# Many-head cross-attention: order of the work ahead of the bundles; expert layer: place of one wait

## The reference

```python
def _L1_ffn_ref(x, uzman_embeddings, W1, b1, W2, b2, onbellek_durumu):   # 8 experts, hidden 512
    sim = tokens @ uzman_embeddings.T                 # the best 7 of 8 experts by sim ...
    scores = einsum('nld,nd->nl', local_embs, t_norm) + 0.1 * onbellek_durumu[local_idx]
    top_scores, top_local = top_k(scores, 2)          # ... and of them the best 2 by score
    weights = softmax(top_scores)
    h = gelu(einsum('nd,edh->enh', tokens, W1) + b1)
    out_all = einsum('enh,ehd->end', h, W2) + b2      # weighted sum of the two chosen

def _L2_xattn_ref(query, key, value, mask, W_q, W_k, W_v, W_o):          # 16 heads of 8
    Q, K, V = _split(query @ W_q.T), _split(key @ W_k.T), _split(value @ W_v.T)
    scores = einsum('bhqd,bhkd->bhqk', Q, K) / sqrt(8)
    scores = where(mask, -inf, scores)                # one mask of 64 x 1601 for all batches
    out = einsum('bhqk,bhkd->bhqd', nan_to_num(softmax(scores)), V)
    return merged(out) @ W_o.T
```

## Time and profile before

| What | Value |
|---|---|
| Time, median of 3 runs | 3037.8 us (3036.95 to 3038.14) |
| The profiled execution: own time / span | 3035.62 us / 3033.8 us |
| Busy: PE, DVE, ACT, POOL | 86%, 67%, 46%, 14% of the span |
| Mean granted clock of PE | 0.928 |
| Expert layer | 713.1 to 973.8 us of the span |
| Many-head stage | 974.1 to about 2196 us of the span |

### The profile page before, as it was taken

One profiled execution on the slowest core, in us unless ns is written; L12 is line 12 of the kernel. 1 busy time (PEld: TensorE's weight loads), 2 busy tenths in 40 slices (PEclk: granted clock), 3 DMA queues, 4 the chain that ended last, 5 costly groups with the idle time before them and its releaser, 6 DMA issues. The chain is left out here.

```text
span 3033.8 us, 66495 instructions
## 1 busy us (share of the span) xinstructions
PE 2614.7 (86%) x26984; PEld 1711.9 (56%) x27014; DVE 2036.0 (67%) x6815; ACT 1385.4 (46%) x2520; POOL 429.6 (14%) x299
## 2 busy tenths in 40 slices
PE   7998645898998999999999999999947989888634
PEld 5767543555776666656556565555624555555423
DVE  5553514675212499999989999899667876556776
ACT  3441312564333255555555555555338964334511
POOL 0000030440000000000000000000005960563200
PEclk9999776898999999999999999999978999999866
DMA  7970410000001000000000001000002210991000
GB/s 235 332 245 3 130 48 19 9 3 17 15 22 37 22 24 23 27 32 24 23 24 24 23 24 34 24 23 2 5 12 79 96 58 1 325 366 66 2 0 14
DMA packets 73344, 189.00 MB, mean 62 GB/s; under 512 B 12130, under 2 KB 39717, under 8 KB 73008
## 3 DMA queue, kind: packets, MB, share of 16 engines
q1 hardware_dynamic: 64912, 156.68, 15.8%
q10 hardware_dynamic: 7104, 26.23, 2.4%
q0 software_dynamic: 1024, 1.85, 0.2%
HBM read 154.19 MB, written 30.79 MB: 61 GB/s over the span
## 5 line engine op out<-in xcount | busy, mean ns | idle before, releaser
L3062 DVE CUSTOM_DVE_ANT_0 L_xattn_junk<-L_xattn_ps_mx,L_xattn_shift 128x512 f32<-128x512 f32 (+1 forms) x1024 | 545.1, 570 | 112.3 <-issue 102.1
L3143 ACT ACTIVATE L_xattn_pT<-L_xattn_ps_st 128x512 f32<-128x512 f32 x768 | 417.0, 594 | 402.4 <-PE L_xattn_ps_st L2901 402.4
L2914 PE MATMUL L_xattn_ps_mx<-L_xattn_kT,L_xattn_qb 32*128 32x512 f32 (+1 forms) x2048 | 480.0, 551 | 0.0
L2901 PE MATMUL L_xattn_ps_st<-L_xattn_qb,L_xattn_kT 32*128 32x256 f32 (+1 forms) x3328 | 454.5, 383 | 0.0
L3108 DVE TENSOR_TENSOR L_xattn_pT<-L_xattn_pT,L_xattn_capT 128x512 f32<-128x512 f32 (+1 forms) x710 | 423.2, 637 | 29.8 <-ACT L_xattn_pT L3143 26.8
L2901 PEld LDWEIGHTS L_xattn_ps_st<-L_xattn_qb,L_xattn_kT 32*128 32x128 f32 (+1 forms) x3328 | 299.3, 180 | 18.5
L2961 PE MATMUL L_xattn_ps_pv<-L_xattn_pT,L_xattn_v 128*17 128x128 f32 x6656 | 263.0, 276 | 0.0
L2961 PEld LDWEIGHTS L_xattn_ps_pv<-L_xattn_pT,L_xattn_v 128*17 128x17 f32 x6656 | 146.1, 96 | 163.3 <-issue 76.1
L2927 PE MATMUL L_xattn_ps_st<-L_xattn_less,L_xattn_ones_b 3*128 3x512 bf16 x768 | 177.8, 385 | 0.9 <-ACT L_xattn_pT L3143 0.7
L2868 POOL TENSOR_TENSOR L_xattn_qb<-ln_sq,L_xattn_four 128x256 f32<-128x256 f32 x32 | 19.6, 615 | 1089.0 <-PE L_xattn_ps_st L2901 1069.3
L2914 PEld LDWEIGHTS L_xattn_ps_mx<-L_xattn_kT,L_xattn_qb 32*128 32x128 f32 x2048 | 151.5, 183 | 23.9 <-DVE L_xattn_tops L3062 14.6
(11 more groups left out here) (615 smaller groups left out, 5030.4 us busy)
## 6 DMA issues: line engine op xcount, KB each, us to landing
L_xattn_ctxT<-context_turned SPq DMA_DIRECT2D x64, 800.5 KB, 6.5
context_turned<-L_xattn_ctxT SPq DMA_DIRECT2D x32, 800.5 KB, 9.7
L_xattn_ctx<-in_ctx SPq DMA_DIRECT2D x32, 768.0 KB
L_xattn_ctx<-in_ctx ACTq DMA_DIRECT2D x32, 768.0 KB
L_attn_cc<-scratch_rows SPq DMA_DIRECT2D x32, 512.0 KB, 3.7
L_xattn_out_keys<-scratch_q SPq DMA_DIRECT2D x32, 200.1 KB, 10.0
L_ffn_w<-in_L_ffn_w SPq DMA_DIRECT2D x4, 1024.0 KB, 10.2
L_ffn_w<-in_L_ffn_W SPq DMA_DIRECT2D x16, 256.0 KB, 3.2
```

Of the source, the lines that this page charges most:

```text
L2901: last = nc.tensor.matmul(st[0:chunk[j], w % 3, 256 * c2:256 * c2 + 256], kT[n % 3][r:r + 32, P * j:P * j + chunk[j]], qb[n % 3][r:r + 32, ...
L2914: last = nc.tensor.matmul(mx[:, w % 3, to:to + width], qb[n % 3][32 * g:32 * g + 32, 2 * (p % 2):2 * (p % 2) + 2, :].rearrange("p h q -> p ...
L3062: last = nc.vector.tensor_tensor_reduce(out=junk[:, w % 3, to:to + width], in0=mx[:, w % 3, to:to + width], in1=shift[:, k0:k0 + width], s ...
L3143: nc.scalar.activation(pT[b % HELD][:, :, gi, :], st[:, w % 3, :].rearrange("p (c k) -> p c k", c=2), ACT.Exp)\
```

## The change

In the expert layer VectorE's wait for `loaded`, with the `bonus` multiplication behind it, stands behind `ln_vector` and no longer ahead of it.

In the many-head stage VectorE's part of the normalisation and the four query reads stand ahead of the wait for `loaded` and the mask work; "set" is now its last step ahead of the loop. TensorE makes the eight units of batch 0 directly behind the query products, in a loop of their own over four PSUM banks (the three of `st`, and `pv`) with a wait only for the unit four back, and only then the transposes of `cap`. ScalarE copies the eight units ahead of `capT`. The loop of bundles starts at -18 on the three engines. Nothing is computed in another way.

```diff
@@ routed_experts, vector
             nc.vector.memset(ones[:, :], 1.0).then_inc(V.did("ones"), 1)
+            ln_vector(c, dve, V, A, PE, tp)
             dve.wait_ge(loaded, 80)
             nc.vector.tensor_scalar(bonus[:, :], te[:, :], 0.1, None, ALU.mult).then_inc(V.did("bonus"), 1)
-            ln_vector(c, dve, V, A, PE, tp)
@@ many_head_cross_attention
+        FIRST_BATCH = [(PREPARED[i][0], 0, PREPARED[i][1]) for i in sorted(PREPARED)]
+        four_banks = [st[:, 0, :], st[:, 1, :], st[:, 2, :], pv[:, :]]
@@ tensor
-            pe.wait_ge(*V.at("q3"))
+            pe.wait_ge(ctx_in[0], 16)
+            for i, (kind, _, m) in enumerate(FIRST_BATCH):
+                bank = four_banks[i % 4]
+                if i >= 4:
+                    pe.wait_ge(prep_read, i - 3)
+                if kind == "V":
+                    for j in range(4 * m, 4 * m + part[m]):
+                        to = P * (j - 4 * m)
+                        last = nc.tensor.matmul(bank[0:chunk[j], to:to + P], ctxT[:, 0, P * j:P * j + chunk[j]], wv[:, :],
+                                                start=True, stop=True)
+                else:
+                    width = SPANS[m][1]
+                    last = nc.tensor.matmul(bank[:, 0:width], wk[:, :], ctxT[:, 0, 512 * m:512 * m + width], start=True, stop=True)
+                last.then_inc(prep_done, 1)
+            pe.wait_ge(*V.at("set"))
             pe.wait_ge(filled, 5)
+            pe.wait_ge(prep_read, 8)
             for j in range(KC):
                 last = nc.tensor.transpose(st[0:chunk[j], j // 8, S * (j % 8):S * (j % 8) + S], cap[0:S, P * j:P * j + chunk[j]],
                                           c.ident[0:S, 0:S])
...
-                    for _ in range(8 if b < -LEAD else 6):
+                    for _ in range(6):
...
-            for b in range(FIRST, LAST):
+            for b in range(-LEAD, LAST):
@@ vector
+            ln_vector(c, dve, V, A, PE, tp)
+            for i in range(4):
+                dve.wait_ge(*PE.at(f"q{i}"))
+                nc.vector.tensor_scalar(qT[:, 512 * i:512 * i + 512], qps[i], DH ** -0.5, None, ALU.mult).then_inc(V.did(f"q{i}"), 1)
             dve.wait_ge(loaded, 144)
...
             nc.vector.memset(zero_b[:, :], 0.0).then_inc(V.did("set"), 1)
-            ln_vector(c, dve, V, A, PE, tp)
-            for i in range(4):
-                dve.wait_ge(*PE.at(f"q{i}"))
-                nc.vector.tensor_scalar(qT[:, 512 * i:512 * i + 512], qps[i], DH ** -0.5, None, ALU.mult).then_inc(V.did(f"q{i}"), 1)
@@ scalar
-            act.wait_ge(*PE.at("capT"))
-            nc.scalar.copy(capT[:, 0:8, :], st[:, 0, :].rearrange("p (j q) -> p j q", q=S))
...
+            for unit in FIRST_BATCH:
+                taken(unit)
+            act.wait_ge(*PE.at("capT"))
+            nc.scalar.copy(capT[:, 0:8, :], st[:, 0, :].rearrange("p (j q) -> p j q", q=S))
...
-            for b in range(FIRST, LAST):
+            for b in range(-LEAD, LAST):
```

More of the change, by code:

```diff
@@ L2780, in many_head_cross_attention @@
         qps = [mx[:, 0, :], mx[:, 1, :], mx[:, 2, :], prep[:, :]]
-        V = Steps(s.sem("vector_steps"), (1, ["set"] + LN_V + [f"q{i}" for i in range(4)]))
+        V = Steps(s.sem("vector_steps"), (1, LN_V + [f"q{i}" for i in range(4)] + ["set"]))
         A = Steps(s.sem("scalar_steps"), (1, LN_A + ["capT"]))
@@ L2815, in many_head_cross_attention @@
         assert len(prep_at) == 12 * B
+        FIRST_BATCH = [(PREPARED[i][0], 0, PREPARED[i][1]) for i in sorted(PREPARED)]
+        assert [prep_at[unit] for unit in FIRST_BATCH] == list(range(1, 9))
+        four_banks = [st[:, 0, :], st[:, 1, :], st[:, 2, :], pv[:, :]]
         def of_bundle(b):
@@ L3154, in taken @@
                 width = SPANS[m][1]
+                bank = prep if n or kind == "M" else four_banks[FIRST_BATCH.index(unit) % 4]
                 if kind == "K":
-                    nc.scalar.copy(kT[n % 3][:, 512 * m:512 * m + width], prep[:, 0:width]).then_inc(prep_read, 1)
+                    nc.scalar.copy(kT[n % 3][:, 512 * m:512 * m + width], bank[:, 0:width]).then_inc(prep_read, 1)
                 elif kind == "V":
@@ L3159, in taken @@
                     nc.scalar.copy(v[n % 3][0:k, 4 * m:4 * m + part[m], :, 0:16],
[L3160 removed]
+                                   bank[0:k, 0:P * part[m]].rearrange("p (j h d) -> p j h d", j=part[m], d=16)).then_inc(prep_read, 1)
                 else:
                     nc.scalar.copy(less[n % 2][:, :, :], prep[:, 0:256].unsqueeze(1).broadcast_to([P, 2, 256])).then_inc(prep_read, 1)
[L3164 removed]
+            for unit in FIRST_BATCH:
+                taken(unit)
+            act.wait_ge(*PE.at("capT"))
+            nc.scalar.copy(capT[:, 0:8, :], st[:, 0, :].rearrange("p (j q) -> p j q", q=S))
+            nc.scalar.copy(capT[:, 8:12, :], st[:, 1, 0:4 * S].rearrange("p (j q) -> p j q", q=S))
+            nc.scalar.copy(capT[0:KREST, 12, :], st[0:KREST, 1, 4 * S:5 * S]).then_inc(A.did("capT"), 1)
+            for b in range(-LEAD, LAST):
                 now = of_bundle(b)
```

6 lines of the change are left out of this document (1 added, 5 removed).

## The result

| | before | after |
|---|---|---|
| Median (range; runs) | 3037.97 us (3036.95 to 3038.69; 4) | 3009.68 us (3008.67 to 3015.64; 4) |
| Profiled execution: own time / span | 3035.62 / 3033.8 us | 3009.04 / 3007.2 us |
| Mean granted clock | 0.928 | 0.931 |

The ratio is 0.9911, with a 95% interval of 0.9896 to 0.9927: faster by 28.3 us in the medians and 26.6 us in the profiled executions.

A forecast was written before the change was run, and what follows sets the result against it. TensorE fills the bundle loop, so the edits' worth is decided at two stage starts: 3.4 us (expert layer) plus 20.6 us (many-head) is 24.0, and 3037.8 - 24.0 = 3013.8 us; range 3010.5 to 3019.0, 8 in 10.

The forecast's parts named there:

- Expert layer: Expert layer's start: normalisation begins behind `ones`, not behind the load and `bonus`; 3.4 us earlier, bounds 0 to 3.5.
- Rival C: Expert layer: the edit gives nothing because another wait sets when the blocks start; 3017.2 us, chance 0.08.
- Normalisation ahead of the masks: Many-head stage's start: VectorE's normalisation starts 8.95 us earlier, less 0.7 us for GpSimd's fills beside its first tiles.
- the hold by the fills: Many-head normalisation: GpSimd's value-tile fills hold up VectorE's first normalised tiles by 0.7 us, bounds 0 to 2.3.
- Rival A: Many-head normalisation: the fills hold VectorE to their end, 2.3 us in place of 0.7; 3015.4 us, chance 0.13.
- Units in four banks: Many-head stage: units follow the last query product, 0.92 us per key and 0.96 per value unit; `cap` transposes 7.0 us later.
- Transposes and copies of cap: Many-head stage, now ahead of bundle -18: 2.13 us as before, with first maxima at 998.56.
- Bundles: Many-head loop: fourteen bundles with 112 fillers gone; from bundle -18 on TensorE's queue is row for row as before.
- Mask work beside the units: Many-head stage: the 2.67 us of mask work goes behind the query reads and runs beside TensorE's eight units.
- Rival B: Many-head queries and units: TensorE's low clock reaches into them, up to +9.3 us; whole 3023.1, half 3018.4; chance 0.12.
- Rival D: Queries, units and bundles from -18 on: slower, TensorE stays at the low clock; 42.1 us, time 3055.9, chance 0.02.

The follow-up runs named there:

- expert_only: The kernel before with only the expert layer's edit (normalisation ahead of the wait for the load and `bonus`): 3031.59 us, ratio 0.9981.
- pool_reads: The changed kernel with a GpSimd copy of 1536 columns of x, read by nobody, behind its first fill of the value tiles: 3006.14 us, one execution.
- norm_only: The kernel before with only VectorE's many-head order changed (normalisation and query reads ahead of the masks), one bank, bundles from -32: 3032.77 us, ratio 0.9988.
- banks_only: The kernel before with only the eight units moved ahead of `cap` in four banks, loop from bundle -18: 3029.19 us, ratio 0.9969.
- one_bank: The changed kernel with all eight units through one bank, each waiting for the copy of the one ahead: 3016.80 us, ratio 0.9927.
- pool_fills: The changed kernel with an extra GpSimd fill of 1536 columns, read by nobody, behind its first fill of the value tiles: 3012.64 us, one execution.
- pool_gap: The pool_reads kernel with GpSimd waiting behind its copy until VectorE's first pair of normalised tiles is written: 3014.02 us, one execution.

## Why the prediction was right, and where not

Direction, place and mechanism were right: two normalisations start at once, the units overlap the masks, and fourteen bundles of transposes go. The steps one by one, measured on the trace of after:

- *Expert layer*, 3.4 us: 3.5 in expert_only, so cost and place were right, and 4.0 in the changed kernel. The start is right (713.87, behind `ones`). From `ones` to the last copy it is 9.30 us (713.79 to 723.09) and was 13.58 (713.17 to 726.75); 3.5 of these 4.3 us are the start, and 0.8 is the clock, which rose some 3 us sooner in this trace than in seven others with the same code; 0.45 of it reaches the end of the layer. That part is luck. Rival C falls.
- *Normalisation ahead of the masks*, 8.95 us less 0.7: the first variances come at 0.03 us from the stage's start (9.05 before), and the last copy ends at 10.42 (19.67 before), 9.25 earlier, where 8.95 less 0.7 were forecast. The term that was mis-sized is the hold by the fills: 0.10, not 0.7, and by luck of phase. Rival A, the full hold, didn't happen in this kernel, but its mechanism is real: in pool_reads the tiles waited for every fill, and the first maxima came 3.0 us later.
- *Units in four banks*: the first at 14.69 us from the stage's start (15.38 forecast; of the 0.69 the hold is 0.6). Pitches are 0.86 us (K) and 0.89 (V), not 0.92 and 0.96: I had taken the time from a unit to the filler behind it, and from unit to unit it is shorter. To the transposes of `cap` it is 6.45 us, not 7.0. No bank was waited for.
- *Transposes and copies of cap*: 2.04, not 2.13.
- In sum the first maxima stand at 23.18, against 24.5 forecast: 21.95 us gained, not 20.6. The 1.3 us between are the hold (0.6), the units (0.55), `cap` (0.09), and 0.1 that I can't put down to one step.
- *Bundles*: 43.03 us from there in both. As forecast.
- *Mask work beside the units*: hidden, as forecast, but longer: the short pieces of `shift` and `cap` took 0.61 us each (0.19 before), and GpSimd's three `qb` 3.86 (1.75 before). I had costed them at their lengths alone, and left out that they now meet. norm_only shows what it costs when TensorE waits: 3.56 us in place of 2.67.
- *Rival B*, the low clock in queries and units, didn't come: the stretch of the units stood at 1.00.

```profile
985.39:991.84 6.45, 5.81 (x35) 4.16 (x34) 4.33 (x8) 3.79 (x8) 3.86 (x3) 1.00 0.00 0
```

- *Rival D*, a low clock in the bundles, didn't come in this trace either, but in part in four others with the same bundles (banks_only, one_bank, pool_fills, pool_gap: 1.6 to 4.8 us). I gave it 0.02 as a whole stretch of 42 us; what exists is a smaller one, some microseconds in some executions. Whether it explains the run of 3015.64 us is open.

In numbers: the two stages gave 25.9 us where 24.0 were forecast (0.6 expert layer, 1.3 head), and about 1.1 of these 1.9 is luck, the moment of the clock's rise and the phase of the first tile; 0.7 came from elsewhere in the two profiled executions; and 1.7 is that the medians lie 28.3 apart and these two executions 26.6. So of the 4.1 us by which the time was missed, 2.4 are not the two stages'. The range was too narrow at its lower end, because all of its width was given to costs and none to the terms that could be over-priced, or to the spread of executions.

## What to carry to other kernels

At the start of a stage, put first what needs only data that is already there, and let work that waits for a load follow behind it; but check who waits for the work put off, since here each of two moves alone gave far less at the first maxima (3.05 and 12.6 us) than both (21.95). Through one bank, eight dependent units cost 6.0 us more than through four. Unread work that keeps the clock up is worth trimming piece by piece, not all at once: in the traces with all of it gone the clock fell and the gain with it, and in that with only the later half kept 4.6 us were gained.
